# First loads reordered, dense experts over four pairs of banks, and new places: a Mamba and mixture-of-experts kernel on one core

## The chip, the cores and the metric

The kernel runs on one core of a Trainium2 chip. Its time is the device time of one execution in microseconds (us), the median of several; lower is better. The engines are TensorE (PE in the profile; PEld is its weight load), VectorE (DVE), ScalarE (ACT), GpSimd (POOL) and SyncE (SP), whose queue starts most of the transfers (SPq; ACTq is ScalarE's). Each engine runs its own instructions in program order and waits at semaphores for the others.

## The reference

32 sequences (batches) of 512 tokens, 256 features, float32 throughout.

```python
h = x + mamba(layernorm(x)*g1 + b1)        # in_proj 256->1024, conv of 4 taps, silu,
                                           # x_proj, softplus(dt), scan of 16 states per
                                           # channel over the tokens, D, gate silu(z), out_proj
m = layernorm(h)*g2 + b2
x = layernorm(x + h + gelu(m @ w1.T + b1) @ w2.T + b2)

scores = softmax(x @ gate.T)               # 8 experts, the best 2 of each token
routed = sum over the chosen: weight * down_e(silu(gate_e(x)) * up_e(x))
shared = down_s(silu(gate_s(x)) * up_s(x))
out = layernorm(x + routed + shared)
```

## The kernel before, in words

**Work of one batch.** The 512 tokens are four tiles of 128. `pre` normalises x (`xt`), projects it, convolves it and computes dt, B and C. `scan` is the centre: for each of the 16 states and 4 channel tiles POOL multiplies dt*x by B (`dBx`, line 587, 128x1024), ACT takes the exponential of dt*A (line 741), DVE runs the recurrence over 512 tokens (`hs`, line 1201), PE turns the result over (line 954), and DVE adds it with weight C (`acc`, line 1217). B is spread over the partitions by a transfer per state (`Bbc`, line 439, four buffers). `post` gates, projects, runs the MLP, the third layernorm, the router and the shared expert, and stores the token sum with the shared result (`shared`, line 821).

**Routed experts.** Tokens are scattered to slots by expert in device memory (`X_slots`, line 622), in groups of 6, 6, 6, 6, 4, 2 and 1 batches; when a group is complete its slots are run two tiles at a time (a pair: loads of `wx` and `xin` at lines 484 and 490, PE, ACT and DVE through one bank psE, result to `Y_slots` at line 506). Before that `Y_slots` is cleared by 114 transfers of 256 KB for each of the first two groups (line 424), and the slots behind the last expert's are filled by two large transfers `X_slots<-xin` (line 413, in `behind`).

**Finishing.** For each batch 0 to 30, SP loads `shared` into `fx` (line 521), after the previous output is stored; POOL gathers the two experts' rows of each of the four token tiles with an adding indirect transfer (line 643, eight in all: four for the first choice, then, when all four have landed, four for the second); ACT sums (line 875), POOL and ACT work out mean and variance (lines 551 to 560, 670), ACT normalises (line 882) and stores (line 885). The single `fx` makes one batch wait for the last.

**Batch 31** has no slots: in `last` all eight experts run on all its tokens (dense). Expert s: four products gate and up (line 1147; a float32 product is two matmul instructions, so eight in the profile), ACT's tanh (line 857), two DVE products (lines 1362, 1365), four down products (line 1154), and four weighted additions into `y_dense` on DVE (line 1376). Two sets of two banks, psA and psH, hold the up products of expert s and later its down products; the up products of expert s + 2 overwrite them and so wait for the additions of expert s. The weights of the eight experts are loaded into buffers that the scans no longer use (line 466); PE's first product waits for all eight. At last `finish` normalises `y_dense` like the others.

**Order.** The order of the instructions of every engine is written out by hand: `AT` holds for each strand of an engine (scan, pre, post, ...) a list of places in ticks, 64 ticks to a batch; `weave` merges the strands by 64*b + place. A place is an order on one engine, not a time: an engine runs ahead as far as its waits allow.

**The start.** SP issues 15 loads of weights, b2 and the shared expert's weights (lines 394 to 396), then `zeros`, the first `X_slots` fill, x of batch 0 (line 403), and the second fill. ACT, PE and DVE wait for all of the weights, ACT and PE also for two small DVE products (`s_halved`).

## Time and profile before

| | us |
|---|---|
| median of 3 runs | 5006.31 (5001.06 to 5010.78) |
| the profiled execution | 4998.19 |
| its span, first to last instruction | 4996.5 |
| granted TensorE clock, mean | 0.952 |

The span has three parts: from 0 to the first recurrence (line 1201) at 90.7 us, the 32 batches' recurrences up to 4814 us, and the rest to 4996.5 us. Busy time is summed over instructions of an engine; instructions that overlap in its pipeline count twice, so a busy share near 1 is full. The bracket behind a row of the timeline gives the idle time ahead of the first of its instructions and what ended it.

### The profile page before, as it was taken

The numbers are of one execution on the slowest core, as the hardware profiler recorded it, in microseconds if no ns is written. First come the engines' busy times: TensorE is split into PE (matmuls) and PEld (weight loads), VectorE is DVE, ScalarE is ACT, GpSimd is POOL, SyncE is SP. The second block draws the span as 40 slices with busy tenths as digits, with TensorE's granted clock in tenths as the row PEclk, the third lists the DMA queues.
The fourth block names the chain that finished last, engine by engine and source line by source line (L and its number), as shares of the span: only waits on it lengthen the run. The fifth ranks groups of instructions, "written<-read, shape, count | busy, mean of one in ns | idle before, by whom it ended". The sixth has DMA issues, their size and how long they took to land. (4 is left out here: it accounts for less than half of the span.)

```text
span 4996.5 us, 76410 instructions
## 1 busy us (share of the span) xinstructions
PE 4150.0 (83%) x21374; PEld 2881.0 (58%) x21374; DVE 4243.0 (85%) x6062; ACT 3574.0 (72%) x6537; POOL 3565.3 (71%) x2235
## 2 busy tenths in 40 slices
PE   2688888888888888888888888888888889888886
PEld 1455555555656665565566656566665566655663
DVE  3899999988999988899988889899888888878752
ACT  3677767777776777777777777777777777776753
POOL 3676677666666667777777777778787886777853
PEclk7899999999999999999999999999998999999988
DMA  5122222243343424333333433333354453555653
GB/s 131 41 85 85 91 87 75 85 145 102 113 138 123 125 91 122 100 105 106 95 103 84 122 102 104 104 96 105 82 145 114 125 132 92 163 141 141 177 154 86
DMA packets 348420, 552.00 MB, mean 110 GB/s; under 512 B 39377, under 2 KB 196178, under 8 KB 347874
## 3 DMA queue, kind: packets, MB, share of 16 engines
q1 hardware_dynamic: 279026, 448.92, 29.8%
q0 software_dynamic: 47616, 65.17, 6.4%
q10 hardware_dynamic: 21360, 33.03, 1.8%
q8 instruction: 177, 2.90, 0.2%
q14 instruction: 241, 1.97, 0.1%
HBM read 432.78 MB, written 181.33 MB: 123 GB/s over the span
## 5 line engine op out<-in xcount | busy, mean ns | idle before, releaser
L587 POOL TENSOR_TENSOR dBx<-dtx,Bbc 128x1024 f32<-128x1024 f32 x1024 | 2445.1, 2448 | 439.9 <-DVE hs L1201 425.6
L1201 DVE TENSOR_TENSOR_SCAN hs<-ps,dBx 128x512 f32<-128x512 f32 x2048 | 2406.6, 1207 | 268.6 <-ACT ps L741 168.5
L741 ACT ACTIVATE ps<-dt,A 128x512 f32<-128x512 f32 x2048 | 1396.2, 689 | 476.4 <-DVE hs L1201 453.5
L954 PE MATMUL ps<-ident,hs 128*128 128x128 f32 x8192 | 1297.3, 292 | 389.1 <-DVE acc L1217 264.3
L954 PEld LDWEIGHTS ps<-ident,hs 128*128 128x128 f32 x8192 | 976.5, 148 | 912.3 <-DVE acc L1217 528.6
L1217 DVE SCALAR_TENSOR_TENSOR acc<-ps,C_tok,acc 128x512 f32<-128x512 f32 x1664 | 1184.1, 734 | 150.7 <-PE ps L954 139.6
L622 POOL DMA_INDIRECT X_slots<-xs,slots x248 | 248.0, 1000 | 356.1 <-DVE slots L1339 295.9
L643 POOL DMA_INDIRECT fx<-Y_slots,slots x248 | 392.4, 1582 | 143.8 <-issue 48.9
L919 PE MATMUL ps<-xnT,w_in 128*128 128x512 f32 x512 | 266.7, 636 | 86.8 <-DVE xc L1190 57.2
L1190 DVE SCALAR_TENSOR_TENSOR xc<-ps,conv_w,xc 128x511 f32<-128x511 f32 (+2 forms) x384 | 284.8, 742 | 61.3 <-ACT xc L705 53.3
L1113 PE MATMUL ps<-xsT,wx 128*128 128x128 f32 x2432 | 312.1, 280 | 16.8 <-ACT xsT L833 15.9
L1113 PEld LDWEIGHTS ps<-xsT,wx 128*128 128x128 f32 x2432 | 294.2, 195 | 35.6 <-issue 34.0
L971 PE MATMUL ps<-xnT,w_in 128*128 128x512 f32 x512 | 277.5, 633 | 0.0
L1018 PE MATMUL ps<-mT,w_m 128*128 128x512 f32 x512 | 236.7, 600 | 25.9 <-ACT mT L787 25.8
L1035 PE MATMUL ps<-w_m,post_tmp 128*128 128x256 f32 x1024 | 257.3, 379 | 0.0
L1002 PE MATMUL ps<-w_out,xc 128*128 128x256 f32 x1024 | 252.5, 379 | 0.0
L571 POOL TENSOR_TENSOR dt<-dt,dtx 128x1024 f32<-128x1024 f32 x64 | 153.2, 2394 | 135.7 <-ACT dtx L732 135.7
L705 ACT ACTIVATE xc<-ps,conv_b,conv_w 128x512 f32<-128x512 f32 x128 | 99.0, 774 | 188.4 <-PE ps L919 188.2
L943 PE MATMUL ps<-few 64*128 64x512 f32 x256 | 159.2, 707 | 54.6 <-ACT dt L727 54.3
L1128 PE MATMUL ps<-wx,ge 128*128 128x256 f32 x608 | 168.6, 400 | 42.1 <-DVE ge L1354 40.0
L1002 PEld LDWEIGHTS ps<-w_out,xc 128*128 128x128 f32 x1024 | 189.6, 190 | 23.2
L1035 PEld LDWEIGHTS ps<-w_m,post_tmp 128*128 128x128 f32 x1024 | 186.8, 190 | 22.0
(209 smaller groups left out, 6262.6 us busy)
## 6 DMA issues: line engine op xcount, KB each, us to landing
Bbc<-B_scratch SPq DMA_DIRECT2D x512, 256.0 KB, 3.8
wx<-in_experts SPq DMA_DIRECT2D x304, 384.0 KB, 3.9
Y_slots<-zeros SPq DMA_DIRECT2D x228, 256.0 KB, 4.4
xin<-X_slots SPq DMA_DIRECT2D x304, 128.5 KB, 3.0
Y_slots<-xin SPq DMA_DIRECT2D x304, 128.0 KB
xt<-in_x SPq DMA_DIRECT2D x32, 512.0 KB, 5.2
shared<-xt ACTq DMA_DIRECT2D x31, 512.0 KB, 3.1
fx<-shared SPq DMA_DIRECT2D x31, 512.0 KB, 4.5
```

The lines of the kernel that those rows point to most:

```text
L587: pool.tensor_tensor(dBx[u % 3][:], dtx[b % 2][:, 2 * h:2 * h + 2, :], Bbc[g % NBB][:, n % CH:n % CH + 1, :].broadcast_to([P, 2, T]), ALU. ...
L643: pool.indirect_dma_start(out=fx[:, t, :], out_offset=None, in_=Y_slots[g % 2], in_offset=bass.IndirectOffsetOnAxis(ap=slots[:, f % NKEPT, ...
L741: act.activation(psA[s % 2][:], dt[b % 2][:, j, :], ACT.Exp, scale=A[:, j, n:n + 1]).then_inc(s_dA, 1)
L919: i = pe.matmul(bank(b, j)[:], w_in[:, k, j * P:(j + 1) * P], xn[:, k, :], start=(k == 0), stop=(k == KD - 1))
L954: i = pe.transpose(psH[w % 2][:, j * P:(j + 1) * P], hs[(n * CT + j) % NHB][:, t * P:(t + 1) * P], ident[:])
L971: i = pe.matmul(psG[j % 2][:], w_in[:, k, DI + j * P:DI + (j + 1) * P], xn[:, k, :], start=(k == 0), stop=(k == KD - 1))
L1002: i = pe.matmul(psG[q][:, t * D:(t + 1) * D], c[:, k, (2 * q + t) * P:(2 * q + t + 1) * P], w_out[:, k, :], start=False, stop=(k == CT - 1))
L1035: i = pe.matmul(psG[q][:, t * D:(t + 1) * D], post_tmp[:, k, (2 * q + t) * P:(2 * q + t + 1) * P], w_m2[:, k, :], start=False, stop=(k == ...
L1113: i = pe.matmul(psE[:, o * HALF + m * P:o * HALF + (m + 1) * P], w[:, m, (2 * k + o) * P:(2 * k + o + 1) * P], xsT[:, (m * KD + k) * P:(m ...
L1190: dve.scalar_tensor_tensor(out=c[:, j, s:], in0=bank(b, j)[:, 0:T - s], scalar=conv_w[:, j, NK - 1 - s:NK - s], in1=c[:, j, s:], op0=ALU.m ...
L1201: dve.tensor_tensor_scan(hs[s % NHB][:], psA[s % 2][:], dBx[s // 2 % 3][:, s % 2, :], 0.0, ALU.mult, ALU.add).then_inc(s_scan, 1)
L1217: dve.scalar_tensor_tensor(out=o, in0=psH[w % 2][:], scalar=C_tok[b % 2][:, t, n:n + 1], in1=o, op0=ALU.mult, op1=ALU.add).then_inc(s_weig ...
```

## The change

- x of batch 0 is issued first of all. The weights are in two parts: the first nine loads (`FIRST_WEIGHTS`, to D) and the rest. ACT, PE and DVE wait for the first part alone; the rest is waited for where it is first used (ACT and PE at the first gating of batch 0, DVE at its first shared expert). A's negation stands right behind its exponential; POOL waits for no weights.
- The two `X_slots` fills move from the start to places 224 and 410 (batches 3 and 6). Twelve of the nineteen clears of `Y_slots` that stand at batch 0 move ahead of its B rows (and likewise for each later batch).
- Dense experts: up products go to psA and psH in turn, down products to (psP, psE) and psG in turn. Up of expert s waits for the DVE products of expert s - 2; down of expert 0 waits for the routed pairs' last results, of expert 1 for the shared sum and the router, and of later ones for the additions two experts back.
- Loads of the dense weights stand earlier on SP.
- Batches 28 and 29 finish in `acc`, batch 30 in its own `xt`, where the sum already is: no store and load for it. The loads for 28 and 29 wait for no output.
- One semaphore per token tile for the gathers: the second choice of tile t waits for the first choice of tile t, ACT's sum of tile t for its own two.
- Batch 31's last mean and variance come from DVE (`bn_stats`, `bn_aggr`, the lines that batch by batch serve the third layernorm) instead of ACT sums and squares.
- All places of `AT` are drawn anew.

```diff
 AT = {
...
-    "SP_behind": [-85.339, -71.224, -50.752],
-    "SP_clear": [-11.769, 15.931, 15.931, 16.906, 16.906, 16.906, 16.906, 17.299, 90.454, 92.69, 94.379, 94.936,
-        95.538, 95.644, 95.793, 97.504, 97.504, 98.305, 102.83],
-    "SP_last": [27.951, 32.597, 62.166, 79.006, 105.65, 134.4, 141.109, 142.785],
+    "SP_behind": [-60.8412, 224, 410],
+    "SP_clear": [-60.8312, -58.5583, -55.8551, -50.6302, -41.323, -41.323, -38.9959, -24.0274, -23.8632, -22.6523,
+        -14.3152, -11.0408, -1.9789, 74.0528, 77.6396, 80.6374, 83.0428, 84.4844, 105.8878],
+    "SP_last": [22.4349, 24.0079, 24.074, 33.4011, 54.077, 56.4291, 65.501, 66.0845],
...
-        ps_dense, y_dense = [psA, psH], xt[(NB - 1) % NX_IN]
...
+        ps_up, ps_down, y_dense = [psA, psH], [(psP, psE), psG], xt[(NB - 1) % NX_IN]
+
+        def to_finish(f):
+
+            if f >= NB - 2:
+                return xt[f % NX_IN]
+            return acc[f % 2][:, :, 0:D] if f >= NB - 4 else fx
...
+        NFIRST = 9
+        FIRST_WEIGHTS, ALL_WEIGHTS = 16 * NFIRST, 16 * (len(loads) - NFIRST + 2)
...
-            return 2 * NTB * 16 * (b + 1)
+            return 2 * 16 * (b + 1)
...
-            for dst, key_ in loads:
+            def rows(b):
+                sp.dma_start(xt[b % NX_IN][:], a["x"][b].rearrange("(t p) d -> p t d", p=P)).then_inc(
+                    s_x_in[b % NX_IN], 16)
+
+            rows(0)
+            for dst, key_ in loads[:NFIRST]:
                 if key_ == "dt_proj_w":
                     sp.wait_ge(s_few, 1)
-                sp.dma_start(dst if key_ == "dt_proj_w" else dst[:], a[key_]).then_inc(s_weights, 16)
+                sp.dma_start(dst if key_ == "dt_proj_w" else dst[:], a[key_]).then_inc(s_first, 16)
+            for dst, key_ in loads[NFIRST:]:
+                sp.dma_start(dst[:], a[key_]).then_inc(s_weights, 16)
             sp.dma_start(b2, a["mlp_b2"]).then_inc(s_weights, 16)
             sp.dma_start(w_shared[:], a["experts"][NE]).then_inc(s_weights, 16)
...
-                            sp.wait_ge(s_gathered, gathers(first[before[g]] + groups[before[g]] - 1))
+                            for t in range(NTB):
+                                sp.wait_ge(s_gathered[t], gathers(first[before[g]] + groups[before[g]] - 1))
...
-                        if f == NB - 1:
+                        if f >= NB - 2:
                             continue
                         sp.wait_ge(s_kept, 16 * (f + 1))
-                        if f:
+                        if f >= NB - 4:
+                            sp.wait_ge(s_y_turned, NB * CT)
+                        elif f:
                             sp.wait_ge(s_stored, 16 * f)
-                        sp.dma_start(fx[:].rearrange("p t d -> p (t d)"), shared[f]).then_inc(s_fx_in, 16)
+                        sp.dma_start(to_finish(f)[:], shared[f].rearrange("p (t d) -> p t d", d=D)).then_inc(s_fx_in, 16)
...
-            pool.wait_ge(s_halved, HALVED)
...
+                                    if f == NB - 2:
+                                        pool.wait_ge(s_sum, (f + 1) * 2)
+                                    else:
+                                        pool.wait_ge(s_fx_in, 16 * (f + 1))
                                     for k in range(NR):
...
-                                if (c, t) == (1, 0):
-                                    pool.wait_ge(s_gathered, gathers(f) - NTB * 16)
+                                if c:
+                                    pool.wait_ge(s_gathered[t], gathers(f) - 16)
...
-                                    out=fx[:, t, :], out_offset=None, in_=Y_slots[g % 2],
+                                    out=to_finish(f)[:, t, :], out_offset=None, in_=Y_slots[g % 2],
                                     in_offset=bass.IndirectOffsetOnAxis(ap=slots[:, f % NKEPT, c, t:t + 1], axis=0),
-                                    compute_op=ALU.add).then_inc(s_gathered, 16)
-                        yield b
-                        yield from normed("fin", f, s_var_fin, s_rstd_fin, s_norm_fin, b)
+                                    compute_op=ALU.add).then_inc(s_gathered[t], 16)
...
+                        if f < NB - 1:
+                            yield from normed("fin", f, s_var_fin, s_rstd_fin, s_norm_fin, b)
+                            continue
+                        pool.wait_ge(s_norm_fin, f * NTB)
+                        pool.wait_ge(s_mean_post, (NB + 1) * NTB)
+                        pool.tensor_scalar(ve["fin"][:], mv[:, :, 1], EPS, None, ALU.add).then_inc(s_var_last, 1)
+                        pool.tensor_scalar(nb["fin"][:], mv[:, :, 0], -1.0, None, ALU.mult).then_inc(s_var_last, 1)
+                        pool.wait_ge(s_var_last, 2)
+                        pool.tensor_tensor(rs["fin"][:], ve["fin"][:], m_half[:], ALU.pow).then_inc(s_rstd_fin, 1)
+                        pool.wait_ge(s_rstd_fin, f * 2 + 1)
+                        pool.tensor_tensor(nb["fin"][:], nb["fin"][:], rs["fin"][:], ALU.mult).then_inc(s_rstd_fin, 1)
...
-            act.wait_ge(s_weights, ALL_WEIGHTS)
+            act.wait_ge(s_first, FIRST_WEIGHTS)
             act.activation(A[:], A[:], ACT.Exp).then_inc(s_A_exp, 1)
-            act.wait_ge(s_halved, HALVED)
-            act.wait_ge(s_consts, CONSTS)
+            act.wait_ge(s_negated, 1)
...
+                        if (b, j) == (0, 0):
+                            act.wait_ge(s_weights, ALL_WEIGHTS)
...
-                    if b == NB - 1:
+                    if b >= NB - 2:
...
+                        y = to_finish(f)
+                        if f == NB - 1:
+                            yield from empty(b, 2 * NTB)
+                        else:
+                            for t in range(NTB):
+                                yield b
+                                act.wait_ge(s_gathered[t], gathers(f))
+                                if t == 0 and f:
                                     act.wait_ge(s_less["fin"], f)
...
-                                act.wait_ge(s_summed, (NE - 1) * NTB + t + 1)
-                            act.activation(y[:, t, :], y[:, t, :], ACT.Copy, accum_out=total["fin"][:, t:t + 1]).then_inc(
...
+                                act.activation(y[:, t, :], y[:, t, :], ACT.Copy,
+                                               accum_out=total["fin"][:, t:t + 1]).then_inc(s_total["fin"], 1)
+                            yield from square("fin", f, lambda t: y[:, t, :], b, s_var_fin, lambda t: squared[:])
...
-            pe.wait_ge(s_weights, ALL_WEIGHTS)
-            pe.wait_ge(s_halved, HALVED)
+            pe.wait_ge(s_first, FIRST_WEIGHTS)
             pe.wait_ge(s_consts, CONSTS)
-            pe.wait_ge(s_diag, CT)
...
+                        if (b, j) == (0, 0):
+                            pe.wait_ge(s_diag, CT)
+                            pe.wait_ge(s_weights, ALL_WEIGHTS)
...
+                        if (b, q) == (0, 0):
+                            pe.wait_ge(s_halved, 1)
...
-                            pe.wait_ge(s_summed, (s - 1) * NTB)
+                            pe.wait_ge(s_hidden_d, s - 1)
...
-                                i = pe.matmul(ps_dense[s % 2][o][:], w[:, (2 * k + o) * P:(2 * k + o + 1) * P],
+                                i = pe.matmul(ps_up[s % 2][o][:], w[:, (2 * k + o) * P:(2 * k + o + 1) * P],
...
+                        if s == 1:
+                            pe.wait_ge(s_yo, pairs_to[NG - 2] * 2)
+                        elif s == 2:
+                            pe.wait_ge(s_sum, NB * 2)
+                            pe.wait_ge(s_combined, 3)
+                        else:
+                            pe.wait_ge(s_summed, (s - 2) * NTB)
...
-                            i = pe.matmul(ps_dense[(s - 1) % 2][t // 2][:, t % 2 * D:(t % 2 + 1) * D],
+                            i = pe.matmul(ps_down[(s - 1) % 2][t // 2][:, t % 2 * D:(t % 2 + 1) * D],
...
-            dve.wait_ge(s_weights, ALL_WEIGHTS)
-            dve.tensor_scalar(ws_d, ws_d, 0.5, None, ALU.mult).then_inc(s_halved, 1)
+            dve.wait_ge(s_first, FIRST_WEIGHTS)
+            dve.wait_ge(s_A_exp, 1)
+            dve.tensor_scalar(A[:], A[:], -1.0, None, ALU.mult).then_inc(s_negated, 1)
...
-            dve.wait_ge(s_A_exp, 1)
-            dve.tensor_scalar(A[:], A[:], -1.0, None, ALU.mult).then_inc(s_halved, 1)
-            dve.wait_ge(s_halved, HALVED)
...
+                if (b, q) == (0, 0):
+                    dve.wait_ge(s_weights, ALL_WEIGHTS)
+                    dve.tensor_scalar(ws_d, ws_d, 0.5, None, ALU.mult).then_inc(s_halved, 1)
...
+                for t in range(NTB):
+                    dve.wait_ge(s_summed, (NE - 1) * NTB + t + 1)
+                    if t == 0:
+                        dve.wait_ge(s_var_post, NB * 2)
+                    dve.bn_stats(stats[:, t, :], y_dense[:, t, :]).then_inc(s_bn_post, 1)
+                for t in range(NTB):
+                    dve.wait_ge(s_bn_post, NB * NTB + t + 1)
+                    dve.bn_aggr(mv[:, t, :], stats[:, t, :]).then_inc(s_mean_post, 1)
```

## Rows read from the trace of the kernel before

**Rows 1.** The page: span, and busy time of two engines.

```profile
span 4996.5 us, 76410 instructions
...
PE 4150.0 (83%) x21374; PEld 2881.0 (58%) x21374; DVE 4243.0 (85%) x6062; ACT 3574.0 (72%) x6537; POOL 3565.3 (71%) x2235
```

**Rows 2.** Busy PE, PEld, DVE, ACT, POOL by stretch; clock, DMA share, GB/s.

```profile
0.00:37.00 37.00, 0.00 (x0) 0.00 (x0) 4.34 (x89) 1.83 (x3) 2.80 (x44) 1.00 0.98 232
...
1000.00:2000.00 1000.00, 862.22 (x4531) 600.78 (x4531) 897.53 (x1247) 731.29 (x1283) 686.57 (x402) 0.97 0.39 120
```

**Rows 3.** Timeline of the start: start us, duration us, engine, line.

```profile
10.11 13.26 SPq L403 DMA_DIRECT2D xt<-in_x  x1
14.58 0.26 ACT L656 ACTIVATE A<-A 128x64 f32<-128x64 f32 x1 [12.48 <-DMA w_shared<-in_experts]
...
36.70 0.42 ACT L684 ACTIVATE dtx<-xt 128x256 f32<-128x256 f32 x1 [21.87 <-DMA xt<-in_x]
...
90.70 2.34 DVE L1201 TENSOR_TENSOR_SCAN hs<-ps,dBx 128x512 f32<-128x512 f32 x2 [28.14 <-POOL dBx L587]
```

**Rows 4.** Transfers of the first 60 us: GB/s in 40 slices of 1.5 us; issues with KB and us to landing.

```profile
GB/s 0 100 328 341 193 310 272 249 392 378 230 214 208 204 217 186 206 178 158 157 220 282 312 240 221 242 215 201 206 149 212 195 189 189 129 36 0 0 0 0
...
X_slots<-xin SPq DMA_DIRECT2D x2, 3598.0 KB, 27.7
...
xt<-in_x SPq DMA_DIRECT2D x1, 512.0 KB, 26.5
```

**Rows 5.** DVE's costliest groups, 1197 to 3378 us, 15 batches: busy, mean ns, idle before.

```profile
L1201 DVE TENSOR_TENSOR_SCAN hs<-ps,dBx 128x512 f32<-128x512 f32 x960 | 1130.0, 1207 | 99.1 <-ACT ps L741 87.0 <-PE ps L954 6.4 <-issue 2.9
...
L1217 DVE SCALAR_TENSOR_TENSOR acc<-ps,C_tok,acc 128x512 f32<-128x512 f32 x781 | 555.5, 733 | 70.1 <-PE ps L954 65.2
```

**Rows 6.** SP's transfers in batch 3 (timeline): a load of B.

```profile
541.25 0.33 SPq L439 DMA_DIRECT2D Bbc<-B_scratch  x1
```

**Rows 7.** Timeline of the end.

```profile
4876.42 0.33 SPq L521 DMA_DIRECT2D fx<-shared  x1
...
4880.15 1.64 POOL L643 DMA_INDIRECT fx<-Y_slots,slots  x1 [10.28 <-DMA Y_slots<-xin]
...
4882.07 0.38 DVE L1231 BATCH_NORM_AGGREGATE mv<-stats 128x2 f32<-128x6 f32 x4
...
4885.58 0.25 POOL L599 TENSOR_SCALAR ve_post<-mv 128x4 f32<-128x4 f32 x1
...
4909.30 0.38 PE L1076 MATMUL ps<-ident,mT 128*128 128x128 f32 x2
...
4915.01 0.43 SPq L466 DMA_DIRECT2D xt<-in_experts  x1
...
4920.63 8.99 PE L1147 MATMUL ps<-mT,dt 128*128 128x512 f32 x16 [10.96 <-DMA xt<-in_experts]
...
4942.42 3.70 PE L1147 MATMUL ps<-mT,dtx 128*128 128x512 f32 x8 [1.98 <-DVE xt L1376]
...
4973.72 3.70 PE L1147 MATMUL ps<-mT,xt 128*128 128x512 f32 x8 [1.97 <-DVE xt L1376]
...
4981.58 1.66 DVE L1376 SCALAR_TENSOR_TENSOR xt<-ps,r,xt 128x256 f32<-128x256 f32 x4 [0.52 <-PE ps L1154]
...
4984.74 0.42 ACT L875 ACTIVATE xt<-xt 128x256 f32<-128x256 f32 x1 [0.51 <-ACT fx L882]
...
4991.01 2.07 ACT L882 ACTIVATE xt<-xt,nb_fin,rs_fin 128x256 f32<-128x256 f32 x4 [1.71 <-POOL nb_fin L560]
```

**Rows 8.** Dense experts by step: us, PE busy, granted clock, DMA share, GB/s.

```profile
4933.30:4942.40 9.10, 7.12 (x16) 0.81 0.21 29
4942.40:4949.80 7.40, 5.43 (x16) 1.00 0.23 77
```

**Rows 9.** POOL's gathers from 4910 us on; DVE's statistics, 1197 to 3378 us.

```profile
L643 POOL DMA_INDIRECT fx<-Y_slots,slots x16 | 25.0, 1561 | 26.7 <-DMA fx<-shared 18.1 <-DMA fx<-Y_slots,slots 4.9 <-issue 3.7
...
L1227 DVE BATCH_NORM_STATS2 stats<-ps 128x6 f32<-128x256 f32 x60 | 22.5, 417 | 0.0
```

153 lines of the change are left out of this document (72 added, 81 removed), and 41 rows, old and new, of the table AT.

## Prediction

> **What bounds the kernel now.** I read the page's head first, then the busy time by stretch, then the two ends and the middle of the timeline. The page gives the span and says that DVE and PE are the fullest engines [rows 1]. By stretch the picture splits: in the first 37 us nothing but the transfers is busy (DMA share 0.98, PE 0), and in a middle stretch of 1000 us DVE is busy 897.5 us, doubly counted overlaps included [rows 2]. So the kernel is three problems: a start that waits for transfers, 32 batches in which DVE sets the pace, and an end that is one chain.
>
> The start: ACT's first work on x begins at 36.70 us, released by the load of x. That load was issued at 10.11 us and its issue alone took 13.26 us, as it stood behind a 3.6 MB fill of `X_slots`; it landed 26.5 us after issue [rows 3, 4]. From there to the first recurrence at 90.70 us runs one chain of batch 0. The end: PE finishes batch 31's shared expert at 4909.7, stands still until the last dense weights, issued at 4915.01, are there at 4920.6, and then works the dense experts in steps, each ending with an idle 1.97 us "<-DVE xt", the additions that free a bank [rows 7]. The last additions end at 4983.24, and another 13.3 us go for the last layernorm and store.
>
> **Start: x first, two parts of weights.** The nine first loads and x come to 0.52 (x) + 1.05 (in_proj) + 0.18 (the small ones) = 1.75 MB; all weights of before are 3.2 MB. Adding up the 1.5 us slices of [rows 4]: 1.44 MB have moved by 7.5 us, 1.91 by 9.0, 3.09 by 13.5. So 1.75 MB are reached at 8.5 us and 3.2 MB at 13.8. Before, ACT started 0.8 us after that point (14.58) [rows 3]. First part ready: 8.5 + 0.8 = 9.3 us. Then the exponential (0.26), the negation on DVE (like it, 0.2) and two hand-overs, 0.3 together: ACT reaches x, long landed, at 10.1. It was 36.70: **26.6 us less**. Everything to the first recurrence hangs on that chain; POOL and PE are free, and later weights have 30 us to land. Next in line could be B's rows, behind twelve clears of 256 KB: they can start when `zeros` has landed, near 17 us, and 3.1 MB at the 200 GB/s of the later slices take 16 us, done by 33 us; the rows are written some 33 us after ACT's start, at 44. Hidden, with 10 us to spare. Bounds: the first part ready at 8.0 to 12 us, so 24 to 28 us less.
>
> The Trainium skill ("DMA: Bandwidth & Descriptors", Anatomy of one DMA) puts a transfer at 2 us plus its bytes at 436 GB/s; by that 1.75 MB would be there at 0.8 + 6.0 = 6.8 us and the gain 2.5 us more. The slices here never came near that rate over the first 9 us (1.91 MB, 212 GB/s), so I keep the rows' figure.
>
> **The fills moved into batches 3 and 6.** Each now stands between two loads of B on SP. A load of B can be issued when the buffer four states back is free, three states before its use; 15 batches of 16 states took 2181 us [rows 5], 9.1 us a state, so 27 us of slack. Alone, 3.6 MB at some 210 GB/s take 17 us, and the load of B behind it 4 more: 21 us, hidden. Two in line took 27.7 us to land [rows 4]; with 4 more that is 32 us, and 5 us would show, twice. The load that would stand behind the fill in batch 3 was issued at 541.25 with no wait of POOL on it [rows 6]. Bounds 0 to 10 us, taken +1.
>
> **Dense experts over four sets.** A clean step is 7.40 us: PE busy 5.43 at clock 1.00; a slow one 9.10 with PE busy 7.12 at 0.81 [rows 8]. The 1.97 us of idle in each is the wait for the additions. Now up of expert s waits for the DVE products of s - 2. These follow the up products by 0.6 (tanh) + 1.4 (two products), while PE has 3.5 us of the next up products to do; additions (1.65 us) fall beside them; DVE has 3.1 us and ACT 0.6 us in a step of 5.43. So PE sets the step. From the first up at 4920.63 to the last at 4973.72 were 53.1 us for seven steps; now 7 x 5.43 = 38.0. That is **15.1 us less**, of which 3.4 + about 1.8 is the clock: two later slow steps and part of the first one ran at 0.81 to 0.85, after PE had stood idle. The Trainium skill ("TensorE: Matmul & The Clock Gate", Part 1) says that the array's rate is released by activity and falls back after idling; by that rule all seven steps run at the full 2.4 GHz. If the slow steps stayed, the gain would be 10 us. From the last up to the last addition nothing changes (9.5 us).
>
> **The dense phase starts earlier.** The weights are loaded before the scans end, so the 10.9 us from 4909.7 to 4920.6 go: next in line are batch 31's own shared products, right ahead on PE. **10.6 us less.** The first down products wait for the last routed pair, which in the new order stands ahead on PE but whose second ACT eviction stands behind the first dense tanh: that costs only waiting of batch 30's gathers.
>
> **The gathers that held batch 31's layernorm.** POOL took 4880.15 after 10.28 us of waiting; the row blames a store, but `fx`'s load was issued at 4876.42, once the previous output was out, and lands then. Three gathers stood ahead of L599, which came at 4885.58 [rows 7]; DVE's statistics were ready by 4882.7 [rows 7]. Batch 28 now has a buffer of its own and gathers earlier: **2.9 us less**. Bounds 0 and 5.
>
> **Last layernorm.** Before: 1.5 us in which ACT was still with batch 30, then 4.64 us of sums, mean and squares up to POOL's variance, then power, normalising and store. Now four `bn_stats` at 0.42 [rows 9] and `bn_aggr`, 2.1 us, and 0.25 more on POOL. 1.5 + 4.6 - 2.4 = **3.7 us less**.
>
> **What becomes late instead.** Batch 30's finish: its gathers stand behind batch 29's mean on POOL, which waits for ACT past the fourth dense tanh, near 4931; eight gathers of 1.56 with 0.30 between take 15 us [rows 9], landed at 4950. ACT takes them after the last tanh (4951): sums 2.0, mean, squares 2.5, power 1.7, normalising 2.1: done at 4961, while batch 31's scale is ready at 4959 to 4961. The two chains end together; I take 2 us off the gain. Tail: 15.1 + 10.6 + 2.9 + 3.7 - 2 = **30 us less**, bounds 15 and 36. Gather waits by tile save POOL its 2.4 us per batch where POOL is not the bound: nothing.
>
> **Places drawn anew.** This is the part with no row. In the middle DVE's two main groups waited 99.1 + 70.1 us in 15 batches, 11.3 us a batch [rows 5]; that bounds a gain (350 us over 31 batches, never all), and a loss of the same size is as possible. Merging both sets of places for one middle batch, I find POOL's order unchanged, 30 of DVE's 153 steps moved by at most three places, 36 of ACT's 166 and 20 of PE's 151 by at most five. That is nearest to no change: I take 0, with 1 us a batch either way, +-30.
>
> **Sum.** -26.6 + 1 - 30 + 0 = -55.6. Against the profiled execution (4998.19) that is 4942.6; the median of the runs shown is 8.1 above it, so 5006.3 - 55.6 = **4950**.
>
> **Rivals.**
> (a) The forecast, 4920 to 4975: 0.60.
> (b) The new order takes waits out of the recurrences, over 1 us a batch: ACT's exponentials alone are waited for 87 us in 15 batches. Against: few steps move. 4950 - 32 to 60, say 4912: 0.15.
> (c) It costs about 1 us a batch. For: on DVE the new order keeps recurrences together more (11 instead of 9 a batch stand third or later in a run), and each waits for an exponential that needs the bank of two before. 4950 + 32 = 4982: 0.11.
> (d) The end's gain is half: batch 30's gathers and ACT's part of batch 29, between the fourth and fifth tanh (7.5 us against a step of 5.4), hold the dense chain. +15: 4965: 0.08.
> (e) Slower: the same mechanism as (c), exponentials and PE's turns late at the runs of recurrences and additions on DVE, at more than 1.8 us a batch; from there 32 batches eat the 56 us, and at 2.3 us the time is 5024. Against: the 13 us to be doubled are mostly waits the order cannot move. 0.06.
>
> A difference under 0.2% (10 us) can't be told from none. (a) to (d) are all faster than 4996; (e) lies partly within. Faster 0.92, same 0.03, slower 0.05. Range, 8 in 10: 4918 to 4984.
>
> **What would show it.** Right: ACT's first L684 near 10 us and the first recurrence near 64; the last recurrence to the end in about 152 us instead of 183; dense steps of 5.4 us at clock 1.00 with no idle "<-DVE"; 145 us a batch in the middle as before. Wrong: a first L684 after 13 us; DVE waiting for a load of B in batches 3 or 6; idle before L1201 in the middle more than 1 us a batch away from 6.6; a last ACT chain that waits for `Y_slots` gathers.

## The result, and the profile after

The changed kernel takes **4893.4 us** (median of 4, 4885.8 to 4901.2) where the kernel before, beside it on the same chip, takes 5008.6 (4 runs): ratio **0.976**, 95% interval 0.973 to 0.979. The forecast was 4950, its range 4918 to 4984: right in sign, half of the gain missed, outside the range. The profiled execution took 4885.84 us, 112 under the one before, and its span divides like this:

| us | before | after | change | forecast |
|---|---|---|---|---|
| start, to the first recurrence | 90.7 | 66.4 | -24.3 | -26.6 |
| first to last recurrence | 4723.7 | 4673.1 | **-50.6** | **+1** |
| of it batches 0 to 6 / 7 to 11 | 960 / 723 | 960 / 723 | 0 / 0 | |
| of it batches 12 to 24 / 25 to 31 | 1900 / 1141 | 1883 / 1107 | -17 / -34 | |
| last recurrence to the end | 182.1 | 144.6 | -37.5 | -30 |

A batch is counted from its first recurrence to the next one's. The first gather of a finishing step comes in batch 13. The page of after, answering [rows 1]; the line numbers are those of the changed kernel from here on (recurrence L1245, additions of states L1261, exponential L776, gathers L669, dense up and down L1186 and L1200, tanh L894):

```profile
span 4884.1 us, 76499 instructions
...
PE 4105.8 (84%) x21374; PEld 2848.5 (58%) x21374; DVE 4258.4 (87%) x6070; ACT 3579.8 (73%) x6521; POOL 3566.1 (73%) x2235
```

The timeline of its start, answering [rows 3]:

```profile
0.82 0.45 SPq L407 DMA_DIRECT2D xt<-in_x  x1
...
6.01 0.47 SPq L414 DMA_DIRECT2D D_col<-in_D_param  x1
...
11.80 0.26 ACT L692 ACTIVATE A<-A 128x64 f32<-128x64 f32 x1 [9.70 <-DMA D_col<-in_D_param]
12.40 0.42 ACT L719 ACTIVATE dtx<-xt 128x256 f32<-128x256 f32 x1 [0.34 <-DVE A L1219]
...
66.42 2.34 DVE L1245 TENSOR_TENSOR_SCAN hs<-ps,dBx 128x512 f32<-128x512 f32 x2 [28.17 <-POOL dBx L610]
```

From ACT's first work on x to the first recurrence it is 54.0 us in both kernels: the whole gain is that ACT starts at 12.4 and not at 36.7.

DVE's two main groups in the 15 batches from 1170 to 3341 us, answering [rows 5]:

```profile
L1245 DVE TENSOR_TENSOR_SCAN hs<-ps,dBx 128x512 f32<-128x512 f32 x961 | 1127.1, 1207 | 90.1 <-ACT ps L776 75.6 <-issue 5.6 <-PE ps L988 4.5
L1261 DVE SCALAR_TENSOR_TENSOR acc<-ps,C_tok,acc 128x512 f32<-128x512 f32 x781 | 554.4, 736 | 79.6 <-PE ps L988 73.9
```

Together they waited 169.7 us, and 169.2 before. Inside that sum the recurrences' waits for exponentials fell from 87.0 to 75.6 us, and the additions' waits rose from 70.1 to 79.6. Another wait shrank more, that of DVE's first product of a routed pair for ACT. Its row in the same 15 batches, before and then after:

```profile
L1351 DVE SCALAR_TENSOR_TENSOR ge<-ge,ps 128x256 f32<-128x256 f32 x71 | 28.7, 404 | 19.4 <-ACT ge L838 19.4
```

```profile
L1398 DVE SCALAR_TENSOR_TENSOR ge<-ge,ps 128x256 f32<-128x256 f32 x71 | 28.8, 405 | 4.7 <-ACT ge L875 4.7
```

All of DVE's idle time in these batches fell from 225.3 us (2181.0 less 1955.7 busy) to 209.6 (2171.0 less 1961.4). Overlapping instructions count once in such a busy time, not twice as the text ahead of the prediction says: 960 recurrences of 1207 ns are 1159 us and stand as 1130. What the middle gained is told with e1 and e11. The end, answering [rows 7]:

```profile
4828.99 7.03 PE L1186 MATMUL ps<-mT,dt 128*128 128x512 f32 x16
4835.86 1.89 PE L1200 MATMUL ps<-dt,hs 128*128 128x256 f32 x8
4837.59 3.60 PE L1186 MATMUL ps<-mT,dtx 128*128 128x512 f32 x8
...
4863.55 3.60 PE L1186 MATMUL ps<-mT,xt 128*128 128x512 f32 x8
...
4871.30 1.66 DVE L1423 SCALAR_TENSOR_TENSOR xt<-ps,r,xt 128x256 f32<-128x256 f32 x4 [0.52 <-PE ps L1200]
4872.88 1.39 DVE L1430 BATCH_NORM_STATS2 stats<-xt 128x6 f32<-128x256 f32 x4
4874.19 0.36 DVE L1433 BATCH_NORM_AGGREGATE mv<-stats 128x2 f32<-128x6 f32 x4
...
4876.64 0.25 POOL L679 TENSOR_SCALAR ve_fin<-mv 128x4 f32<-128x4 f32 x1 [2.19 <-ACT xt L918]
...
4878.62 2.07 ACT L918 ACTIVATE xt<-xt,nb_fin,rs_fin 128x256 f32<-128x256 f32 x4 [2.07 <-POOL nb_fin L684]
```

No bracket stands behind these rows of PE. Its one wait, 0.40 us, is before the last down product, the clock stays at 1.00, and a step takes 5.16 us. From the first up product to the last addition it is 44.0 us, 62.6 before.

### The profile page after: what moved, and what is told of

It reads as the page before. It is cut to its first block and busy times, and to the rows that moved or that the text cites. A ratio compares the mean times of both kernels' runs of the same rounds, so it can differ in the third digit from the quotient of the medians.

```text
span 4884.1 us, 76499 instructions
## 1 busy us (share of the span) xinstructions
PE 4105.8 (84%) x21374; PEld 2848.5 (58%) x21374; DVE 4258.4 (87%) x6070; ACT 3579.8 (73%) x6521; POOL 3566.1 (73%) x2235
## 5 line engine op out<-in xcount | busy, mean ns | idle before, releaser
L1245 DVE TENSOR_TENSOR_SCAN hs<-ps,dBx 128x512 f32<-128x512 f32 x2048 | 2399.9, 1207 | 212.9 <-ACT ps L776 122.7
L776 ACT ACTIVATE ps<-dt,A 128x512 f32<-128x512 f32 x2048 | 1393.8, 689 | 435.8 <-DVE hs L1245 388.8
L988 PE MATMUL ps<-ident,hs 128*128 128x128 f32 x8192 | 1271.1, 286 | 466.7 <-DVE acc L1261 345.3
L988 PEld LDWEIGHTS ps<-ident,hs 128*128 128x128 f32 x8192 | 953.7, 145 | 943.6 <-DVE acc L1261 592.5
L1261 DVE SCALAR_TENSOR_TENSOR acc<-ps,C_tok,acc 128x512 f32<-128x512 f32 x1664 | 1181.5, 736 | 161.2 <-PE ps L988 147.4
L669 POOL DMA_INDIRECT fx<-Y_slots,slots x224 | 354.0, 1580 | 70.9 <-issue 41.0
L953 PEld LDWEIGHTS ps<-xnT,w_in 128*128 128x128 f32 x512 | 94.8, 203 | 156.6 <-issue 153.5
```

Source lines behind the costliest of these rows:

```text
L669: pool.indirect_dma_start(out=to_finish(f)[:, t, :], out_offset=None, in_=Y_slots[g % 2], in_offset=bass.IndirectOffsetOnAxis(ap=slots[:, ...
L776: act.activation(psA[s % 2][:], dt[b % 2][:, j, :], ACT.Exp, scale=A[:, j, n:n + 1]).then_inc(s_dA, 1)
L953: i = pe.matmul(bank(b, j)[:], w_in[:, k, j * P:(j + 1) * P], xn[:, k, :], start=(k == 0), stop=(k == KD - 1))
L988: i = pe.transpose(psH[w % 2][:, j * P:(j + 1) * P], hs[(n * CT + j) % NHB][:, t * P:(t + 1) * P], ident[:])
L1245: dve.tensor_tensor_scan(hs[s % NHB][:], psA[s % 2][:], dBx[s // 2 % 3][:, s % 2, :], 0.0, ALU.mult, ALU.add).then_inc(s_scan, 1)
L1261: dve.scalar_tensor_tensor(out=o, in0=psH[w % 2][:], scalar=C_tok[b % 2][:, t, n:n + 1], in1=o, op0=ALU.mult, op1=ALU.add).then_inc(s_weig ...
```

## The experiments

Sixteen kernels ran in four groups, each group on one chip with the kernel before beside it. A ratio is to that one. The median of the kernel before lay between 5011.5 and 5019.3 us in these groups, and at 5008.6 beside the first run of after, so "above after", which compares medians of two groups, is good to some 10 us. Each kernel has one profile. Six kernels (e12, e6, e7, e13, e15 and after) have the same instructions in the same order in batches 7 to 31, and their profiles differ: batches 7 to 11 took 723 to 735 us, 12 to 24 1875 to 1886, 7 to 24 together 2602 to 2619, and 25 to 31 1106 to 1115. Smaller differences in the columns of batches are not read. The table holds what the profiles gave, by part, in us; in brackets are batches 7 to 11 and 12 to 24:

| | ratio (95%) | first recurrence | batches 7-24 | 25-31 | 29, 30 | end |
|---|---|---|---|---|---|---|
| before | 1 | 90.7 | 2622 (723 + 1900) | 1141 | 167, 182 | 182.1 |
| after | 0.976 (0.973-0.979) | 66.4 | 2606 (723 + 1883) | 1107 | 163, 172 | 144.6 |
| e12 after, again | 0.976 (0.974-0.979) | 67.1 | 2604 (724 + 1879) | 1106 | 162, 172 | 142.7 |
| e1 new places on before | 0.997 (0.995-0.999) | 91.4 | 2605 (713 + 1891) | 1146 | 179, 184 | 183.6 |
| e9 the same, waits by tile | 0.986 (0.984-0.988) | 92.2 | 2595 (715 + 1880) | 1118 | 164, 176 | 174.4 |
| e2 old places on after | 0.991 (0.989-0.994) | 69.6 | 2628 (722 + 1906) | 1150 | 168, 182 | 159.4 |
| e5 after, gathers together | 0.992 (0.989-0.994) | 67.6 | 2647 (734 + 1913) | 1145 | 179, 184 | 164.9 |
| e10 after, ACT's alone | 0.986 (0.984-0.988) | 66.7 | 2628 (726 + 1902) | 1134 | 174, 182 | 150.1 |
| e11 before, filler | 0.997 (0.996-0.999) | 88.5 | 2611 (718 + 1893) | 1141 | 166, 181 | 182.4 |
| e6 after, two banks | 0.981 (0.979-0.983) | 67.6 | 2616 (735 + 1881) | 1114 | 163, 173 | 158.7 |
| e8 after, one fx | 0.982 (0.979-0.984) | 67.9 | 2607 (733 + 1874) | 1114 | 166, 173 | 164.2 |
| e7 after, all weights first | 0.980 (0.977-0.982) | 73.2 | 2602 (728 + 1875) | 1112 | 165, 172 | 146.7 |
| e13 after, x behind fills | 0.983 (0.981-0.985) | 92.6 | 2614 (733 + 1881) | 1115 | 164, 174 | 142.6 |

**e1 and e2: places and structure crossed.** The lists of `AT` alone are exchanged:

```diff
 e1 (before):  AT[...] = new, for all strands but SP_behind, SP_clear
 e2 (after):   AT[...] = old, for all strands but SP_behind, SP_clear and the four *_last
```

> The kernel before, with every table of places of the changed kernel except the two of SP that go with the moved fills (SP_behind, SP_clear); loads, banks, buffers and waits stay as before. Theory P (the redrawn places alone took the waits out of the recurrences): first recurrence still at about 91 us, first to last recurrence 4673 +-8 us instead of 4724, batches 25 to 31 together 30 to 35 us shorter; profiled time 4940 to 4952 us. Rival S (the waits went because of the structure: gathers awaited by tile, last sums in buffers of their own): first to last recurrence 4720 to 4730 us and a time of 4990 to 5005 us.

> The changed kernel, with the places of before in every table except SP_behind, SP_clear and the four of the dense experts (ACT_last, DVE_last, PE_last, SP_last); loads, banks, buffers and waits stay as changed. Theory P: the recurrences take 4720 to 4730 us again, the start keeps its 24 us and the end nearly all of its 37; time 4936 to 4945 us. Rival S: recurrences 4673 +-8 us, time 4886 to 4895 us. If both carry a part, this and the run of the new places on the old structure lie between, and their two differences from their base add up to about 50 us.

e1's median was 5000.3 us, e2's 4970.8. Neither theory holds: rival S had the time of e1 (4990 to 5005) and not that of e2 (4886 to 4895), theory P had neither. In batches 7 to 11, before any gather, the changed kernel gains nothing (723 us in both); e1's 713 belongs to five batches that all ran at a granted clock of 1.00; what that is worth is told with e11. From batch 12 on the two parts work together. In batches 12 to 24 the new places alone took 1891 us (e1) and the structure alone 1906 (e2), against 1900; the ten kernels that have new places and waits by tile took 1874 to 1886. In batches 25 to 31 neither part gains alone (1146 and 1150 against 1141) and both together gain 34. Batches 29 and 30 of e1 show what is missing: new places, and then ACT in batch 29 stands before its first sum until all gathers are in, with the pair's `xsT` behind it, PE behind that and DVE behind PE. Its timeline (line numbers of before, moved by 7):

```profile
4444.55 1.57 POOL L650 DMA_INDIRECT fx<-Y_slots,slots  x1 [0.16 <-issue]
...
4448.44 0.42 ACT L882 ACTIVATE fx<-fx 128x256 f32<-128x256 f32 x1 [11.08 <-DMA fx<-Y_slots,slots]
...
4448.85 0.58 ACT L840 ACTIVATE xsT<-ps 128x512 f32<-128x512 f32 x1
...
4449.58 3.75 PE L1120 MATMUL ps<-xsT,wx 128*128 128x128 f32 x16 [10.13 <-ACT xsT L840]
...
4453.78 0.42 DVE L1358 SCALAR_TENSOR_TENSOR ge<-ge,ps 128x256 f32<-128x256 f32 x1 [13.62 <-ACT ge L845]
```

**e3 and e4: one engine's old places.** After, with DVE's old places (e3), and with SP's and POOL's (e4).

> The changed kernel with DVE's places of before alone (all DVE tables but DVE_last). Theory P1 (what helped is where DVE itself takes its products for routed pairs and its additions): 25 to 50 us more than the changed kernel, 4911 to 4936 us. Rival P2 (what helped is that ACT and PE, or SP and POOL, deliver earlier to DVE): within 10 us of the changed kernel, 4880 to 4900 us.

> The changed kernel with SP's and POOL's places of before alone (all but SP_last, SP_behind and SP_clear). Theory P1 (DVE's own order, or ACT's and PE's): within 5 us of the changed kernel, 4881 to 4898 us. Rival P3 (loads of routed weights, stores of results and gathers moved, and with them the finish steps of batches 25 to 31): 20 to 35 us more, nearly all of it in batches 25 to 31, 4906 to 4921 us.

Measured: 5220.4 us (ratio 1.041) and 5014.4 us (0.999). Against after nearly every batch lost, 10 and 3 us on average in batches 7 to 24 and 9 and 2 already in batches 1 to 6. Theory and rival miss in both runs: such a mix prices the mismatch of two orders and says nothing of where the redrawn ones gained.

**e5, e10, e9: the waits by tile.** After, with waits for all four tiles on POOL and ACT (e5), on ACT alone (e10); and e1 with waits by tile added (e9):

```diff
 e5, POOL:  -if c: pool.wait_ge(s_gathered[t], gathers(f) - 16)
            +if (c, t) == (1, 0): the same wait for every tile
 e5, e10, ACT:  -act.wait_ge(s_gathered[t], gathers(f))
                +if t == 0: the same wait for every tile
```

> The changed kernel, but POOL waits before the second half of its gathers, and ACT before its first sum, until the gathers of all four tiles have landed, as before the change. Theory G (the new places only pay in batches 29 to 31 because a sum can start when its own tile is there; with the places on the old kernel one wait of 11 us on ACT, handed on as 13 us on DVE, stood in batches 29 and 30 each): batch 29 back to 175 to 179 us (163 now), batch 30 to 180 to 184 (172 now), batches 1 to 28 within 5 us in all; time 25 +-8 us above the changed kernel, 4903 to 4919 us. Rival F (those waits came from the one buffer fx and the load into it): within 5 us of the changed kernel, 4881 to 4899 us.

> The changed kernel, but only ACT waits for all four tiles before its first sum; POOL's gathers still wait by tile. Theory A (the costly part is ACT standing in its queue with the routed pairs behind it): most of the loss of the run with both waits returns, batches 29 and 30 at 172 us or more and 178 us or more, time 4925 to 4960 us. Rival B (it is POOL that stands before its second half and holds the state products behind it): within 8 us of the changed kernel, 4880 to 4901 us.

> The kernel before with the places of the changed kernel (all but SP_behind and SP_clear) and, on top, the gathers awaited by tile on POOL and ACT; loads, banks and buffers as before. Theory G (the new places pay in batches 29 to 31 only when a sum can start with its own tile): batches 25 to 31 together 1107 to 1118 us, where the places alone gave 1145.5; first to last recurrence 4676 to 4692 us; start 91 us and end 175 to 184 us as before; profiled time 4945 to 4965 us. Rival F (own buffers or the moved fills are needed too): batches 25 to 31 stay at 1138 us or more, time 4980 to 5000 us.

Measured: 4975.3, 4940.8 and 4941.8 us. Theory G holds in direction in all three: without the waits by tile batches 29 and 30 are back at 179 and 184 us, with one wait of DVE of 13.85 us in the first; with them added to e1 they fall to 164 and 176. ACT's wait alone makes 27 of the 38 us in batches 25 to 31. G was too small, though: e5's median is 82 us above after, not 25. Its profiled execution, the slowest of its four, took 102 us more than that of after: 38 in batches 25 to 31, 20 in the end, and 41 in batches 7 to 24, where I had expected nothing; 10 to 12 of the 41 stand in batches 7 to 11, before any gather, and also in e6 and e8, so they are no effect of the edit. Batches 13 to 22 sum to 1470 us in e5, 1455 in e1 and 1443 in after, so there the waits by tile are worth 1 to 3 us a batch. e9 is the strongest of the three: on the kernel before, new places and waits by tile take first to last recurrence from 4723.7 to 4678.5 us, 45 of the 50.6 that the whole change gained there. The new places alone (e1) took 4716.9.

**e8: one buffer fx.** After, with `to_finish` returning `fx` for batches 28 and 29, loaded after the output before it.

> The changed kernel with the last sums of batches 28 and 29 in the one buffer fx again, loaded once the output before it is out; batch 30's stay in its own rows of x. Rival F of the run with gathers awaited together: batches 29 and 30 lose 10 us each and the end 5 to 8, in all 20 us or more. Theory G: batches 1 to 29 unchanged, batch 30 and what follows up to the dense experts 3 to 10 us longer, as SP stands before the load of batch 28 and POOL's gathers behind it; 4889 to 4903 us.

Measured 4918.4 us, 26 above after; of it 20 in the end. Rival F is wrong on batches 29 and 30 (+3 and +1), theory G on the size. The 7 us more of batches 25 to 31 are not read, as said above. Where it goes stands in the timeline of POOL, ACT and PE of e8, during the dense experts:

```profile
4860.69 1.66 POOL L667 DMA_INDIRECT fx<-Y_slots,slots  x1 [14.33 <-DMA fx<-shared]
...
4872.04 0.42 ACT L909 ACTIVATE fx<-fx 128x256 f32<-128x256 f32 x1 [11.90 <-DMA fx<-Y_slots,slots]
...
4876.11 0.58 ACT L892 ACTIVATE hs<-ps 128x512 f32<-128x512 f32 x1
...
4878.19 3.78 PE L1198 MATMUL ps<-dtx,hs 128*128 128x256 f32 x8 [8.36 <-DVE hs L1410]
4881.76 4.90 PE L1184 MATMUL ps<-mT,xc 128*128 128x512 f32 x8
```

The fourth tanh stands on ACT behind batch 29's sums, these wait for gathers, those for the load of `fx`, that for the previous output. PE stands 8.4 us, and its next products run slower (3.78 and 4.90 us for 1.89 and 3.60, at a granted clock of 0.65 from 4878 to 4887 us). That is rival (d) of the prediction. In e2 the old places bring the same wait, 11.45 us before the down products of the fifth expert; in after it is gone, since batch 29's gathers come at 4828.6 to 4841.7 us and ACT's sums find their tiles there.

**e6: two sets of banks.** After, with `ps_down = [psA, psH]` and up products waiting for `s_summed` as before.

> The changed kernel with the dense experts over two sets of banks, up products waiting for the additions of the expert two before, as before the change. Theory: each dense step waits about 2 us for the additions, and after such waits some steps come at the lower clock (7.4 us a step against 5.2, 9.1 where the clock falls): 14 to 21 us more, 4900 to 4907 us. Rival (the earlier start and the gathers carried the gain of the end, the banks little): under 8 us more, 4886 to 4894 us.

Measured 4917.9 us, 24 above after. The end has 14.1 of it, the low edge of what was expected; 12 more stand in batches 7 to 11 of its profile, as in other kernels with that order. The theory holds by the profile of the end. PE's timeline: each step waits, and two up groups run at 5.40 us:

```profile
4865.41 3.70 PE L1186 MATMUL ps<-mT,dtx 128*128 128x512 f32 x8 [1.98 <-DVE xt L1416]
...
4872.81 5.40 PE L1186 MATMUL ps<-mT,xc 128*128 128x512 f32 x8 [1.97 <-DVE xt L1416]
```

**e7 and e13: the start.** After, with ACT, PE and DVE also waiting for `s_weights` (e7); after with x's first load and `SP_behind` back in their places (e13).

> The changed kernel, but ACT, PE and DVE wait for all weights before their first work on x; x is still loaded first. Theory: ACT's first sum comes 3 us later (all weights and x are 3.7 MB against 1.75 MB, and the start ran at some 300 GB/s by then), the first recurrence at 69 to 71 us, and the time is 3 to 4 us more, 4889 to 4897 us: of the 24 us of the start about 20 are x's own. Rival (the split of the weights carries half of it): 10 to 14 us more.

> The changed kernel with its weights still in two parts, but x's first load and the two fills of X_slots back where they were (SP_behind of before: weights, zeros, first fill, x, second fill). Theory X (what the start gained is x's own: before, it landed 22 us after the weights, and the split of the weights only counts once x is there): first recurrence at 88 to 92 us, the time 22 to 26 us above the changed kernel. Rival W (the two parts carry a third or more of the 24 us): first recurrence at 76 to 84 us. With weights awaited together and x first it was 73.2.

ACT's first sum came at 18.30 us in e7, 5.9 later than in after, and the first recurrence 6.8 later, where 3 and 2.6 to 4.6 were expected. The median, 4908.4 us, is 15 above after, which is nearer to the rival's 10 to 14 than to the theory's 3 to 4; but only 6.8 of it stand at the start, and the other 8 in no one place, within what two groups of runs differ by. The split of the weights carries about 7 of the 24 us, between the two. In e13 ACT stood for x, as this row of its timeline shows:

```profile
8.24 0.26 ACT L691 ACTIVATE A<-A 128x64 f32<-128x64 f32 x1 [6.14 <-DMA D_col<-in_D_param]
37.48 0.42 ACT L718 ACTIVATE dtx<-xt 128x256 f32<-128x256 f32 x1 [28.98 <-DMA xt<-in_x]
```

Theory X holds: with x behind the fills the two parts of weights give nothing (first recurrence 92.6); with x first they give 6 to 7 of the 24 us. The median was 4928.4 us, 35 above after where 22 to 26 were expected; 26 of it stand at the start.

**e11 and e14: the granted clock.** Before (e11) and after (e14) with this in `turn`, for every batch after the first:

```diff
+if m in (10, 11):                                   # of the 64 groups of the batch
+    pe.wait_ge(s_dt_relu, (batch + 1) * CT)         # long past
+    3 or 5 x pe.transpose(psP[...], ident, ident)   # nothing reads it
```

> The kernel before, and in every batch after the first PE transposes the identity 3 times before the 11th and 5 times before the 12th group of state transposes, into a bank that is free there; nothing reads it. It fills 1.2 of the 1.8 us that PE stood idle some 33 us into a batch. Theory C (batches 7 to 24 differ by what clock PE was granted: at 1.00 such a batch takes 143.4 to 143.6 us in both kernels, and before the change the clock fell near 33 us of most of them, after idle stretches of PE): the clock of those stretches stays 1.00, batches 7 to 24 shorten by 10 to 20 us together, time 4978 to 4990 us against 4998. Rival D (PE's idle there has nothing to do with it, or the DVE order itself sets the time): batches 7 to 24 within 5 us of 2622, or longer by the added 1.2 us each, time 4995 to 5035 us.

> The changed kernel with the same idle PE slots filled (3 and 5 transposes of the identity before the 11th and 12th group of state transposes of each batch after the first). Theory C says that the clock no longer falls near 33 us there either; but in the changed kernel three batches with such a fall (20 to 22) took 143.6 to 143.7 us all the same, so its order absorbs most of that: batches 7 to 24 shorter by 0 to 8 us, time within 8 us of the changed kernel. Rival (each fall costs the 1 to 2 us that it cost in the order before): 10 to 20 us shorter.

e11 took 4998.7 us (ratio 0.997; 4988.3 when profiled, where before had 4998.2; 4978 to 4990 expected, 4995 to 5035 by rival D), e14 4900.3 (0.977, interval 0.976 to 0.979). These are windows of batch 7 and of 8 us in it, 32 us after its first recurrence, of before, and then of e11 (us; PE, PEld, DVE, ACT, POOL busy; clock):

```profile
1050.60:1197.10 146.50, 128.09 (x672) 88.94 (x670) 129.92 (x184) 105.95 (x186) 97.69 (x58) 0.97 0.40 123
1082.60:1090.60 8.00, 5.93 (x32) 4.65 (x32) 7.04 (x9) 6.20 (x16) 6.86 (x6) 0.79 0.83 238
1342.90:1486.50 143.60, 123.90 (x672) 86.49 (x670) 129.61 (x184) 106.06 (x186) 97.76 (x58) 1.00 0.39 125
```

```profile
1052.00:1195.60 143.60, 124.75 (x681) 87.39 (x679) 129.63 (x183) 106.05 (x186) 97.74 (x57) 1.00 0.39 125
1084.00:1092.00 8.00, 5.57 (x37) 3.91 (x37) 7.82 (x11) 7.07 (x18) 7.72 (x6) 1.00 0.71 193
```

Batch 9 of before (third row) ran at 1.00 throughout and took 143.6 us; batch 7, the same instructions, 146.5. In e11 none of the twelve batches of that kind (7 to 10, 13 to 16, 19 to 22) falls near 33 us; in before nine do. PE's timeline of before just ahead of such a fall, in batch 7, shows idle time of 0.65 and 1.11 us inside 3 us:

```profile
1082.58 0.66 PE L954 MATMUL ps<-ident,hs 128*128 128x128 f32 x4 [0.65 <-DVE acc L1217]
1084.35 4.54 PE L954 MATMUL ps<-ident,hs 128*128 128x128 f32 x20 [1.11 <-DVE acc L1217]
```

The idle time alone does not decide it. In batch 9 PE stood just as long at the same place, and the clock stayed at 1.00:

```profile
1374.91 0.66 PE L954 MATMUL ps<-ident,hs 128*128 128x128 f32 x4 [0.65 <-DVE acc L1217]
1376.69 1.31 PE L954 MATMUL ps<-ident,hs 128*128 128x128 f32 x8 [1.12 <-DVE acc L1217]
```

Theory C holds for the kernel before as to the falls: the filler keeps them away. Their cost is less sure. Batches 7 to 24 are 11 us shorter by the two profiles (10 to 20 expected), which is less than such a column can differ by. The medians, of 12 and 17 runs, differ by 12.8 us, and the ratio's interval (0.996 to 0.999) makes that 6 to 22 us. Later falls, some 120 us into a batch, stayed. The Trainium skill ("TensorE: Matmul & The Clock Gate", A second HAM failure mode: psum-queue depth-cycling) tells of a kernel whose clock swings because PE idles briefly and often between groups that cycle through banks; the rows of batch 7 agree, those of batch 9 show that it need not come so. For the changed kernel the filler gained nothing, as theory C allowed and its rival did not. Three windows of after, batch 7, batch 20, and 8 us of batch 20 32 us in, say why:

```profile
1026.70:1170.20 143.50, 123.86 (x672) 86.44 (x670) 130.19 (x184) 106.49 (x186) 97.46 (x57) 1.00 0.41 126
2910.00:3053.60 143.60, 124.94 (x672) 87.56 (x670) 130.24 (x183) 112.02 (x206) 111.91 (x69) 0.99 0.37 105
2942.00:2950.00 8.00, 5.78 (x30) 4.33 (x30) 7.54 (x9) 7.03 (x16) 6.99 (x7) 0.79 0.88 233
```

The same fall to 0.79 costs the new order nothing in batches 20 to 22 (143.6 to 143.7 us). So the redrawn places do not make an undisturbed batch of this kind shorter (143.4 to 143.6 us against 143.6). In batch 23, without a fall in either, they do by about 1 us (141.4 in before, 140.1 in e7). What differs more is how long PE is at its lower level: 147 us of batches 7 to 24 in before, in 30 falls, and 96 in after, in 22. Over these 18 batches in thirteen profiles (all but e1, e3, e4, e5 and e10), comparing each batch with the same one of the others, a microsecond at the lower level goes with 0.30 us more of the batch's time. By that the 51 us are worth 15, nearly all that batches 7 to 24 gained. This is a correlation, not an experiment: a late engine can bring both the fall and the longer batch.

**e12, e15, e16: the base again, and a try to beat it.** e15 computes the last scale in `ve`, `nb`, `rs` of "post", which are free, instead of those that batch 30's last step still reads; e16 adds the filler.

> The changed kernel once more, beside the others of this chip, as their base: 4885 to 4901 us. Batches 7 to 11, which ran at 143.5 to 147.9 us in its first profile and at 146.5 to 148.1 us in those of two kernels that differ from it only later, show how much one profile says of them: theory C expects any sum between 717 and 735 us, going with the granted clock.

> The changed kernel, the scale of batch 31's last layernorm computed in buffers that are free by then (those of the layernorm before the experts) instead of the ones that batch 30's last step still reads. POOL's first step then follows the mean (0.3 us instead of 2.4 us after it), ACT normalises batch 31 right behind batch 30: the end 1.8 to 2.2 us shorter, 142.5 us and less against 144.6 and 142.7 us in the two profiles of the changed kernel. Rival (ACT is still busy with batch 30 and nothing is gained): under 0.5 us.

> The changed kernel with both edits, the filled PE slots and the free buffers for the last scale. If each does what the theory says: 2 to 10 us under the changed kernel, 4882 to 4891 us by the median. Rival: the filler costs what it saves, and the time is within 3 us of the changed kernel.

e12: 4892.5 us, batches 7 to 11 together 724 us (717 to 735 expected). e15: 4902.2 us (ratio 0.977, 0.976 to 0.979), e16: 4896.5 (0.977, 0.975 to 0.979). In e15 POOL no longer waits for ACT, and the last normalising step begins 0.46 us after the one before it, in place of 2.07:

```profile
4895.36 0.25 POOL L679 TENSOR_SCALAR ve_post<-mv 128x4 f32<-128x4 f32 x1 [0.20 <-DVE mv L1434]
...
4897.72 2.07 ACT L919 ACTIVATE xt<-xt,nb_post,rs_post 128x256 f32<-128x256 f32 x4 [0.46 <-POOL nb_post L684]
```

That is 1.6 us, less than the 1.8 to 2.2 expected, and it doesn't show in the end as a whole (143.8 us). e16 misses its 4882 to 4891 us and lies 3 us above the changed kernel, as its rival had it. Neither of the two beats the changed kernel measurably.

## Why the prediction was wrong

**The failed step: "Gather waits by tile save POOL its 2.4 us per batch where POOL is not the bound: nothing", and with it the places, "nearest to no change: I take 0".** Each alone is nearly right: the waits by tile under the old places give nothing (e2, batches 25 to 31: 1150 us against 1141), and the new places under the old waits cost 4 us there (e1). Together they gain 34, and 17 in batches 12 to 24, where 0 was forecast too; on the kernel before they take 45 us out of the recurrences (e9). I costed the edit on POOL, where it saves a short wait, and not on ACT, where the first sum stood for eight gathers with the routed pairs' evictions behind it. The new places set POOL's finish steps later (the first item from place 92 to 142) and take the orders of DVE, ACT and PE with them; such an order needs sums that start by tile. Of the 34 us, e9 shows 23 for the two together (1141 to 1118). The other 11 are only a little more than profiles of one order differ by there (1106 to 1115); what is real of them comes with the own buffers and the other edits of after, and no run assigns it (e8's 1114 lies within that spread).

I compared both orders for one middle batch and took that for all. The batches with 7 to 12 pairs and up to three finishes, which have most of the gain, I had not merged at all.

**Batches 7 to 24, -16 where 0 was forecast.** "+-1 us a batch" held the size. All of it stands in batches 12 to 24, where gathers and routed pairs run, and it takes the new places and the waits by tile together. PE's clock has a part that was not among my rivals. [rows 2] showed 0.97 for the middle, and I read it as a constant of the kernel. That the falls which the filler takes away cost the kernel before some 6 to 22 us is shown (e11, by its medians). That the new order gains by having fewer of them is worked out from the batches, not shown: DVE's waits for ACT fell too (exponentials 87.0 to 75.6 us and the pairs' products 19.4 to 4.7 in 15 batches), and with the filler, which took falls away in the old order, those two stood at 86.7 and 19.9.

**Rival (b)** named 4912 and 0.15, and its sum was the closest; the measured time lies between its ends, 4890 and 4918. Its reason is half there: the waits for exponentials fell by 11.4 us in 15 batches, but the additions' rose by 9.5, and that the gain needs the waits by tile it did not say. Rivals (c) and (e) had the new order cost time; nothing of that was seen in after.

**The start, -24.3 for -26.6.** x's own load behaved as said. The mis-sized term is "first part ready: 8.5 + 0.8 = 9.3", worked out from bytes. The slices were also added wrongly: by 13.5 us they give 3.28 MB and not 3.09, so all weights were there at 13.3 us, ACT followed 1.3 us later and not 0.8, and the same working would have given 9.8. It measured 11.8. By 9.0 us 1.89 MB had moved in its slices, but `D_col`, 2 KB and the tenth load in the queue, was issued at 6.01 and landed 5.8 us later. In e13, without x in front, it was issued at 4.57 and landed 3.6 us later, and ACT began at 8.24. So x's place at the front costs 3.6 us, 1.4 of it in issues and 2.1 in the landing; how much of the landing is the rate stays open. The Trainium skill ("DMA: Bandwidth & Descriptors", Anatomy of one DMA), which the prediction set beside its own figure, gives its 2 us and 436 GB/s for transfers that GpSimd issues. These are SP's, and the 6.8 us worked out from it are further off than the rows' 9.3.

**The fills, +1:** POOL never waits for a load of B in batches 3 to 6, and batches 3 and 6 took 138.6 and 142.0 us (136.6 and 146.2 before). Nothing shows.

**The end, -37.5 for -30.** By its terms: dense start and POOL's part, from last recurrence to the first up product, 106.2 to 89.5 us, -16.7 for 10.6 + 2.9. Dense steps and additions, 62.6 to 44.0, -18.6 for 15.1: the forecast step of 5.43 measured 5.16, since up and down groups now follow without a gap, and the first of the seven steps has no down products in it and took 3.4. First up to last up was 34.6 us, where 38.0 was forecast. Last addition to the end, 13.3 to 11.2, -2.1 for 3.7 - 2: batch 30's chain and batch 31's end together, as written, and POOL waits 2.19 us for the first. Rival (d), the dense chain held by batch 29's part, did not come; e8 and e2 show it, at 8.4 and 11.5 us of PE's time, and that it takes the own buffers and the new places to keep it off.

Of the 20 us that e5 loses in the end, e10 has 5.5 with ACT's wait alone; the other 15 come with POOL's. Open stays which strand's new places count, in batches 25 to 31 as in the middle, and how much of the middle's gain is the clock's: e14 does not tell, since other falls came for those that its filler took away, and PE was at the lower level for 96 us of batches 7 to 24 in both. Waits by tile on the kernel before with its own places were not run either; e2, which has the rest of the change too, stands for them.

## What to carry to other kernels

Where an edit loosens a wait and another moves what stands around it, price them as a pair: put the loosened wait into the new order of every engine that issues it, above all the one with work of others queued behind it. And merge the orders of the fullest stretches, not of the typical one: seven of 32 batches had two thirds of what the recurrences gained, and the batches without gathers had none.

If the granted clock of a long stretch is below 1.00, split it by repetition. Equal batches of 143.6 and 146.5 us, with the clock beside each, show a cost that no single wait names. Then take several profiles: here those of one order differ by 12 us over five such batches. For a start of many small loads, count the issues and the landing of the last small one behind the large ones, and not the bytes alone.

## What the runs showed of the hardware that I had not expected

PE's clock fell to its lower level after idle time of 0.65 and some 1.1 us within 3 us, without any single long pause, in nine of twelve batches of the kernel before; in three it stayed after the same idle time. 8 short transposes put there kept it at 1.00 at that place in twelve of twelve. With one program the falls differ between executions: after's runs of 4885.8, 4888.9, 4897.9 and 4901.2 us had mean clocks of 0.963, 0.963, 0.961 and 0.960. In the 52 runs of the kernel before, 4996 to 5040 us, time and mean clock go together too (0.960 to 0.941, correlation -0.86).
